# The first loads and the last batch of an attention stage, reordered, in a decoder layer on one Trainium2 core

## The reference, cut to what matters

```python
x = x + attn(layernorm(x))                      # x: 8 batches, 256 rows, 512 wide; 16 heads of 32
x = x + xattn(ctx, ctx, layernorm(x), ...)      # a convolution along the rows
x = x + ffn(layernorm(x))                       # 12 experts, top 3
# attn: q, k, v = rope(h @ Wq.T + bq), rope(h @ Wk.T + bk), h @ Wv.T + bv
#       only the first 26 and the last 64 of a batch's 256 key rows count
#       softmax(q k / sqrt(32)) @ v, then @ Wo.T + bo
```

## Time and profile before

| | |
|---|---|
| median of 3 runs | 1633.63 us (1633.26 to 1633.86) |
| the profiled execution | 1632.18 us, span 1630.4 us |
| PE busy | 1461.7 us, 90% of the span |
| POOL, DVE, ACT busy | 823.0, 795.1, 661.3 us |
| attention block | 0 to about 330 us of the span |
| first product with data on PE | 24.1 us |
| granted TensorE clock, mean | 0.936 |

### The profile page before, as it was taken

The page is one execution under the profiler, slowest core; times in us unless marked ns, Lnnn a source line. Parts: engine busy times, 40 slices in busy tenths (PEclk is TensorE's granted clock), DMA queues, the critical chain, the costliest instruction groups (busy, mean ns, idle before and its releaser), DMA issues. The chain is left out here.

```text
span 1630.4 us, 27973 instructions
## 1 busy us (share of the span) xinstructions
PE 1461.7 (90%) x7638; PEld 1113.4 (68%) x7639; DVE 795.1 (49%) x1098; ACT 661.3 (41%) x1789; POOL 823.0 (50%) x892
## 2 busy tenths in 40 slices
PE   3899999589997841999999999999999999999956
PEld 1555555357775741888888888888888888888842
DVE  3456656448888568734717443473471734000003
ACT  0545555423322130444444444544444445444420
POOL 2444555044442001576766766767666667565530
PEclk9999999989998555999999999999999999999977
DMA  6000000022233540634525433454452543241115
GB/s 243 3 1 0 0 0 1 1 74 89 83 86 113 208 161 13 188 91 110 142 64 159 106 104 100 103 161 109 103 157 50 160 103 77 50 123 32 26 23 215
DMA packets 75260, 148.08 MB, mean 91 GB/s; under 512 B 8864, under 2 KB 13472, under 8 KB 74720
## 3 DMA queue, kind: packets, MB, share of 16 engines
q1 hardware_dynamic: 59232, 110.36, 21.2%
q0 software_dynamic: 14320, 35.40, 10.6%
q10 hardware_dynamic: 1680, 1.97, 0.4%
HBM read 115.11 MB, written 32.59 MB: 91 GB/s over the span
## 5 line engine op out<-in xcount | busy, mean ns | idle before, releaser
L1481 PE MATMUL ps_h<-w_hi,xh 128*128 x708 | 250.5, 365 | 1.4 <-ACT xh L1407 1.4
L1482 PE MATMUL ps_h<-w_lo,xh 128*128 x708 | 246.0, 359 | 0.0
L1504 PE MATMUL ps_y<-w_hi,hh 128*128 x590 | 240.0, 407 | 4.4 <-issue 4.4
L1309 DVE TENSOR_TENSOR w_lo<-stage,w_hi 128x512 f32 x220 | 224.0, 1018 | 27.0
L1505 PE MATMUL ps_y<-w_lo,hh 128*128 x590 | 233.8, 396 | 0.0
L1360 POOL TENSOR_TENSOR y<-y,b_sb 128x512 f32<-128x512 f32 x59 | 80.6, 1366 | 229.6 <-ACT y L1432 229.6
L1353 POOL TENSOR_TENSOR hl<-h,hh 128x1280 fp32r<-128x1280 f32 x59 | 188.2, 3189 | 15.1 <-ACT hh L1426 15.1
L763 PE MATMUL ps_b<-kv,toe 128*128 128x320 f32 x640 | 175.2, 437 | 6.9 <-POOL kv L724 6.9
L1486 PE MATMUL ps_h<-w_hi,xl 128*128 x708 | 167.0, 357 | 0.0
L1413 ACT ACTIVATE h<-ps_h 128x512 f32<-128x512 f32 x177 | 80.6, 527 | 209.2 <-POOL hl L1353 200.8
L763 PEld LDWEIGHTS ps_b<-kv,toe 128*128 128x128 f32 x640 | 123.1, 192 | 58.9 <-issue 9.2
(11 more groups left out here) (204 smaller groups left out, 2321.2 us busy)
## 6 DMA issues: line engine op xcount, KB each, us to landing
stage<-in_wcat SPq DMA_DIRECT2D x220, 256.0 KB, 3.0
toe<-kpad SPq DMA_DIRECT2D x32, 256.0 KB, 3.2
cc<-in_ctx_rev SPq DMA_DIRECT2D x32, 192.0 KB, 3.1
w_lo<-in_wcat SPq DMA_DIRECT2D x4, 1280.0 KB, 11.5
acc<-zeros POOLq DMA_DIRECT2D x1, 4352.0 KB, 18.1
xs<-in_x SPq DMA_DIRECT2D x4, 1024.0 KB, 13.3
x2d<-xs SPq DMA_DIRECT2D x4, 1024.0 KB, 8.3
xnd<-xn_c SPq DMA_DIRECT2D x16, 256.0 KB, 2.0
```

Of the source, the lines that this page charges most:

```text
L1309: nc.vector.tensor_tensor(lo, stage[:, c % NSTAGE], hi.bitcast(F32), ALU.subtract).then_inc(split_done, 1)
L1481: nc.tensor.matmul(out, x_hi, part(w_hi, e, k * FF + lo, hi - lo), start=(k == 0), stop=False)
L1482: nc.tensor.matmul(out, x_hi, part(w_lo, e, k * FF + lo, hi - lo), start=False, stop=False)
L1504: nc.tensor.matmul(ps_y[:], h_hi, part(w_hi, e, KD * FF + k * D, D), start=(k == 0), stop=False)
```

## The change

At the start, x is loaded in the parts of `X_PARTS` (batch 0; batch 1; batches 2 and 3; batches 4 to 7), with the weights between them; ACT issues the biases only when the constants have landed. The first normalisation's statistics, aggregation and inverse root are taken in three groups (batch 0, batch 1, the rest). The inverse root is a power of -1/2 on POOL (`first_std`) in place of the square root on ACT and the reciprocal on DVE. At the end, the last batch is written out on ACT, DVE and PE: the scores of its second tile go into banks 0 to 3, once these are free, right behind those of its first tile in banks 4 to 7; its second tile's transposed probabilities are evacuated by DVE (`take_pt`) and no longer by ACT. All PSUM tiles become slices of one tile `bank`.

```diff
-        ps_t = psum("ps_t", [P, 512])
-        ps_p = psum("ps_p", [P, 2, 512])
-        ps_s = psum("ps_s", [P, 4, 512])
-        ps_o = psum("ps_o", [P, KD, P])
-
-        x_in = [sem(f"x_in{i}") for i in range(4)]
+        bank = psum("bank", [P, 8, 512])
+        ps_t = bank[:, 0]
+        ps_o = bank[:, 1].rearrange("p (k n) -> p k n", k=KD)
+        ps_p = bank[:, 2:4]
+        ps_s = bank[:, 4:8]
+
+        X_PARTS = ((0, 1), (1, 2), (2, 4), (4, B))
+        x_in = [sem(f"x_in{i}") for i in range(len(X_PARTS))]
...
-            for i in range(4):
-                sp.dma_start(xs[:, 4 * i:4 * i + 4, :], xt[:, 4 * i:4 * i + 4, :]).then_inc(x_in[i], 16)
-            for w, src, s in ((wq, wqT, wq_in), (wk, wkT, wk_in), (wv, wvT, wv_in), (wo, woT, wo_in)):
+
+            def load_x(i):
+                part = slice(TPB * X_PARTS[i][0], TPB * X_PARTS[i][1])
+                sp.dma_start(xs[:, part, :], xt[:, part, :]).then_inc(x_in[i], 16)
+
+            def load_w(w, src, done):
                 sp.dma_start(w[:].rearrange("p (k n) -> p k n", k=KD),
-                             src.rearrange("(k p) n -> p k n", p=P)).then_inc(s, 16)
+                             src.rearrange("(k p) n -> p k n", p=P)).then_inc(done, 16)
+
+            load_x(0)
+            load_w(wq, wqT, wq_in)
+            load_x(1)
+            load_w(wk, wkT, wk_in)
+            load_w(wv, wvT, wv_in)
+            load_x(2)
+            load_w(wo, woT, wo_in)
+            load_x(3)
...
+            act.wait_ge(c_in, 16)
             for t, src in ((bias_q, bq), (bias_k, bk), (bias_v, bv), (bias_o, bo)):
                 act.dma_start(t[:], src.partition_broadcast(P)).then_inc(b_in, 16)
-            act.wait_ge(var_ready, 1)
-            nc.scalar.activation(rstd[:], rstd[:], ACT.Sqrt).then_inc(std_ready, 1)
...
-            batch(B - 1, True, False, True)
-            evac_n(B - 1)
+            b = B - 1
+            exps(b, 0)
+            exps(b, 1, (0,), 0)
+            evac_pt(b, 0)
+            exps(b, 1, (1,), 0)
+            evac_o(b, 0)
+            evac_n(b - 1)
+            evac_o(b, 1)
+            evac_n(b)
...
+            def first_std(n, lo, hi):
+                pool.wait_ge(var_ready, n + 1)
+                r = rstd[:, lo:hi]
+                nc.gpsimd.tensor_tensor(r, r, power[:, lo:hi], ALU.pow).then_inc(std_ready, 1)
+
+            first_std(0, 0, TPB)
+            first_std(1, TPB, 2 * TPB)
             pool.wait_ge(c_in, 16)
             first = Steps(pool, pool_step)
             for j in range(3):
                 rope(0, j, first)
+            first_std(2, 2 * TPB, NT)
             batch(0, False, False)
...
+            steps = Steps(dve, dve_step)
+
+            def stats_of(i):
                 dve.wait_ge(x_in[i], 16)
-                with dve.Fori(4 * i, 4 * i + 4) as t:
-                    nc.vector.bn_stats(stats[:, t], xs[:, t]).then_inc(stats_done, 1)
-            dve.wait_ge(stats_done, NT)
-            for t in range(NT):
-                nc.vector.bn_aggr(mv[:, t], stats[:, t]).then_inc(aggr_done, 1)
-            dve.wait_ge(aggr_done, NT)
-            steps = Steps(dve, dve_step)
-            nc.vector.tensor_scalar(rstd[:], mv[:, :, 1], EPS, None, ALU.add).then_inc(var_ready, 1)
-            dve.wait_ge(std_ready, 1)
-            steps.do(nc.vector.reciprocal(rstd[:], rstd[:]))
-            dve.wait_ge(b_in, 64)
...
+            stats_of(0)
+            variance_of(0, TPB)
+            dve.wait_ge(std_ready, 1)
             normalise(0, 0)
             normalise(0, 1)
+            stats_of(1)
+            variance_of(TPB, 2 * TPB)
+            dve.wait_ge(std_ready, 2)
             normalise(1, 0)
             normalise(1, 1)
-            for j in range(4):
-                add_bias(0, j, bank_qkv0[j])
+            dve.wait_ge(b_in, 64)
+            add_bias(0, 0, bank_qkv0[0])
+            add_bias(0, 1, bank_qkv0[1])
+            stats_of(2)
+            add_bias(0, 2, bank_qkv0[2])
+            stats_of(3)
+            variance_of(2 * TPB, NT)
+            add_bias(0, 3, bank_qkv0[3])
+            dve.wait_ge(std_ready, 3)
             dve.wait_ge(taps_in, 32)
...
-            batch(B - 1, True, False, True, tail)
+
+            def take_pt(f):
+                dve.wait_ge(pt_done, 4 * B - 1 + f)
+                if f == 0:
+                    dve.wait_ge(pv_done, 2 * B - 1)
+                nc.vector.tensor_copy(view(pT[:], f * 8 * P, [[4 * P, 2], [1, 4 * P]]), ps_s[0:NK, 2 * f:2 * f + 2])\
+                    .then_inc(pt_evac_last, 1)
+
+            b = B - 1
+            softmax_top(b, 0, tail)
+            softmax_top(b, 1, tail, 0)
+            variance(b - 1)
+            softmax_sum(b, 0, tail)
+            softmax_sum(b, 1, tail, (0,))
+            normalise_1(b - 1)
+            take_pt(0)
+            softmax_sum(b, 1, tail, (1,))
+            take_pt(1)
+            residual(b, 0, True, tail)
+            evac_n(b - 1)
+            residual(b, 1, True, tail)
...
-            batch(B - 1, True, False, True)
-            n_t(B - 1, 0)
-            n_t(B - 1, 1)
+
+            def four_banks_free():
+                pe.wait_ge(t_evac, t_qk(B - 1, 2) + 1)
+                pe.wait_ge(p_evac, p_wo(B - 2, 1, False) + 1)
+                pe.wait_ge(o_evac, 2 * B - 1)
+
+            b = B - 1
+            scores(b, 0)
+            scores(b, 1, four_banks_free, 0)
+            p_t(b, 0, 0)
+            p_t(b, 0, 1)
+            pe.wait_ge(exp_done, 4 * b + 3)
+            p_v(b, 0)
+            pe.wait_ge(pt_evac, 4 * b + 2)
+            p_t(b, 1, 0)
+            n_t(b - 1, 0)
+            pe.wait_ge(exp_done, 4 * b + 4)
+            w_o(b, 0, True)
+            pe.wait_ge(pt_evac, 4 * b + 3)
+            p_t(b, 1, 1)
+            n_t(b - 1, 1)
+            p_v(b, 1, True)
+            w_o(b, 1, True)
+            n_t(b, 0)
+            n_t(b, 1)
...
```

More of the change, by code:

```diff
@@ L128, in attention @@
         rstd1 = sb("rstd1", [P, TPB])
-        power = sb("power", [P, TPB])
+        power = sb("power", [P, NT])
         turn = sb("turn_a", [P, 1])
@@ L158, in attention @@
         pt_evac = sem("pt_evac")
+        pt_evac_last = sem("pt_evac_last")
         pv_done = sem("pv_done")
@@ L246, in evac_k, with exps @@
                 evac(qkt_done, 3 * b + 3, kT[:], ps_t[:].rearrange("p (k n) -> p k n", k=KD)[:, :, 0:NK])
-            def exps(b, t):
-                for f in range(2):
+            def exps(b, t, halves=(0, 1), at=4):
+                for f in halves:
                     act.wait_ge(nmx_ready, 4 * b + 2 * t + f + 1)
@@ L338, in inverse_std @@
                 pool.wait_ge(var1_ready, b + 1)
-                nc.gpsimd.tensor_tensor(rstd1[:], rstd1[:], power[:], ALU.pow).then_inc(rstd1_ready, 1)
+                nc.gpsimd.tensor_tensor(rstd1[:], rstd1[:], power[:, 0:TPB], ALU.pow).then_inc(rstd1_ready, 1)
             def repeat(b, t):
@@ L373, in _, with variance_of @@
         def _(dve):
-            for i in range(4):
+            steps = Steps(dve, dve_step)
+            def stats_of(i):
                 dve.wait_ge(x_in[i], 16)
-                with dve.Fori(4 * i, 4 * i + 4) as t:
-                    nc.vector.bn_stats(stats[:, t], xs[:, t]).then_inc(stats_done, 1)
-            dve.wait_ge(stats_done, NT)
-            for t in range(NT):
-                nc.vector.bn_aggr(mv[:, t], stats[:, t]).then_inc(aggr_done, 1)
-            dve.wait_ge(aggr_done, NT)
-            steps = Steps(dve, dve_step)
-            nc.vector.tensor_scalar(rstd[:], mv[:, :, 1], EPS, None, ALU.add).then_inc(var_ready, 1)
-            dve.wait_ge(std_ready, 1)
-            steps.do(nc.vector.reciprocal(rstd[:], rstd[:]))
-            dve.wait_ge(b_in, 64)
+                for n in range(TPB * X_PARTS[i][0], TPB * X_PARTS[i][1]):
+                    nc.vector.bn_stats(stats[:, n], xs[:, n]).then_inc(stats_done, 1)
+            def variance_of(lo, hi):
+                dve.wait_ge(stats_done, hi)
+                for n in range(lo, hi):
+                    nc.vector.bn_aggr(mv[:, n], stats[:, n]).then_inc(aggr_done, 1)
+                dve.wait_ge(aggr_done, hi)
+                nc.vector.tensor_scalar(rstd[:, lo:hi], mv[:, lo:hi, 1], EPS, None, ALU.add).then_inc(var_ready, 1)
             def settle():
@@ L419, in softmax_top, with softmax_sum @@
                                             ALU.mult).then_inc(nmx_ready, 1)
-            def softmax_sum(b, t, steps):
-                for f in range(2):
+            def softmax_sum(b, t, steps, halves=(0, 1)):
+                for f in halves:
                     dve.wait_ge(exp_done, 4 * b + 2 * t + f + 1)
@@ L556, in w_o, with scores @@
                 mm.then_inc(wo_done, 1)
-            def scores(b, t):
+            def scores(b, t, free=None, at=4):
                 if t == 0:
                     pe.wait_ge(t_evac, t_qk(b, 2) + 1)
-                pe.wait_ge(pt_evac, 4 * b + 2 * t + 1)
+                if free is None:
```

(12 more changed lines are left out.)

6 lines of the change are left out of this document (3 added, 3 removed).

## The result

| | before | changed |
|---|---|---|
| median | 1633.7 us (1633.26 to 1633.86, 4 runs) | 1616.59 us (1614.73 to 1619.98, 4 runs) |
| profiled execution, span | 1632.18, 1630.4 us | 1614.73, 1612.8 us |

The ratio is 0.9898, 95% interval 0.988 to 0.9916: 17.1 us, where 13.3 were forecast. I compare the two profiled executions, 17.45 us apart.

The account below looks back on a forecast made before the run. The prediction took the attention block's two ends as the bound: the wait for all of x and the last batch's chain. 11.9 + 1.4 = 13.3 us off 1633.63 gives 1620.3 us, range 1617.2 to 1624.5.

Parts of the forecast that it names:

- both mechanisms: Attention block: batch 0 starting without all of x gains 11.9 us; the last batch's reordered scores and evacuation gain 1.4.
- S: Start of batch 0's exponentials on ACT, forecast at 41.8 us instead of 53.68, 11.9 us gained.
- Step (b): Start, DVE: last x lands at 29.8 us, eight statistics take 5.1, twelve aggregations 0.9; POOL starts at 36.2.
- Step (c): Start, POOL: the power over 12 columns takes 2.8 us (0.29 + 12 x 0.207), ending at 39.0.
- Step (d): Start: DVE adds at 39.0 us, `kpad` lands at 40.9, `evac_x(1, 1)` lasts 0.88 to 41.8; the 1.28 table load goes.
- The loop behind keeps its waits and its length.: Behind the start of batch 0's exponentials, the attention loop was claimed to keep its waits and its length.
- PE's 3 us of waiting in batch 0: Batch 0: PE on its own would move 14.8 us earlier, the exponentials 11.9, so PE waits about 3 us.
- The end: Last batch: the last output projection comes at 316.9 us instead of 318.33, 1.4 us gained.
- The rival of the clock: Last batch: PE's lower clock lasts into the output projection, the end gives nothing, 1621.7 us; chance 0.15.
- one of the signs of being wrong that the prediction names: The prediction is wrong if the granted clock is at 0.50 in the loop or at the last batch's projections.
- The median: Whole kernel: the median was put 1.45 us above the profiled execution, so 1620.3 us rather than 1618.9.

Follow-up runs that it names:

- e8_power_twice: The changed kernel with a second power over 12 columns on POOL, on a spare tile, ahead of the third group's; 1619.21 us, ratio 0.9916.
- e10_one_root: The changed kernel with one unread square root of one column on ACT, bringing back the table load ahead of batch 0's exponentials; 1621.2 us, ratio 0.9931.
- e2_end_only: The changed kernel with the start put back as in the kernel before, so only the change at the end remains; 1629.81 us, ratio 0.9982.
- e0_again: The changed kernel timed once more with nothing edited; 1617.64 us, ratio 0.9907 to the kernel before.
- e5_pe_kept_busy: The changed kernel with nine unread matrix products in PE's gaps, at the block's end and the convolution's start; 1614.52 us, ratio 0.989.
- e9_all_and_busy_start: The changed kernel with late power wait, last x ahead of wo, last batch's scores first, nine spare products, and three in batch 0; 1606.65 us, ratio 0.9851.

## Why the prediction was wrong

Its direction, both mechanisms and every link of the chain up to S were right; the sum was 3.8 us short (4.2 between the two profiled executions), by terms that were mis-sized and by one it did not have.

- **Step (b), the landing and the statistics.** Landing 29.14 us, not 29.8; eight statistics in 4.85 us, not 5.1. POOL started at 35.3 instead of 36.2. The price of 0.636 a tile came from twelve rows with a wait among them; four tiles without one took 2.47 us before, 0.62 each, and written out they are 0.61.
- **Step (c), the power over 12 columns.** 2.28 us, not 2.8: 0.158 us a column beyond the first two, not 0.207. The row of one column that I took for the fixed part was an addition's. The estimate by the Trainium skill that I weighed against it (GPSIMD Engine Reference, section 3.1), which has 2.6 cycles an element for a two-input operation, would have been 0.73; the measurement decides against it for a power.
- **Step (d).** `kpad` and the rest of the chain held: issue 0.17 us after the addition, 1.7 to its landing. From `evac_x(1, 1)`'s start to the exponential's it took 0.75 us and not 0.88: the exponential starts before the evacuation has ended, which the table load did not do. With (b) and (c) S came to 40.26 and not 41.8: 1.5 of the missing us. e8_power_twice and e10_one_root show that the power and the dropped table load stand on this path in full, and the 11.10 us from the last x to the exponentials in six profiles that the landing does. A part of this term is chance: the landing moved by 1.9 us between executions of the same loads.
- **"The loop behind keeps its waits and its length."** This step failed. Behind S the changed kernel gained another 1.34 us, 1.19 of it in batch 0. The profile of before had PE itself as a second bound there: its q projections, 8.58 us long at the low clock, ended just before both halves' transposes, which ran back to back. e2_end_only, with the same start, had 7.41 us and a batch 0 of 30.16. Of these 1.1 us PE gives 0.33 directly; the other 0.8 is DVE's division of the second tile, 1.77 us long behind POOL's start and 0.96 ahead of it. The changed kernel has the same two differences (0.34 at the k projection, 0.91 for the division). So 1.1 us of the gain is the kernel before having had a long stretch at 1.2 GHz in the profiled execution; whether its other executions had it no trace shows.
- **PE's 3 us of waiting in batch 0.** They did not appear. PE's own part moved by 15.05 us (q projections from 51.20 to 36.15), and its q projections, again at the low clock (8.95 us), filled the time until the first transposes of the probabilities at 44.94.
- **The end.** 2.0 us instead of 1.4: 24 exponentials took 7.46 us (281.25 to 288.71) and both `evac_pt` 1.99, where I had 7.57 and 2.1, and neighbours on ACT overlap, so the first output projection came 0.4 us earlier; from there to the last one it was 7.75 us, not 7.9. The rival of the clock was real: at 0.50 into the projections in e0_again, it took 4.0 us, more than the end brings. I had it at 0.15; of the changed kernel's three profiles it was one. That is also one of the signs of being wrong that the prediction names.
- **Behind the block.** The sum ended there. The profiles have another 0.9 us: 0.4 lost where the convolution starts and 0.7 won in it (181.99 us, 182.68 before), where the granted clock left 0.50 sooner behind its first product, and 0.6 in the feed-forward part, whose cause is open.
- **The median.** I put it 1.45 us above the profiled execution, as before; it was 1.86 above. Over the twelve executions of the changed kernel the median is 1616.7, and its gains over the kernel beside it were 17.1, 14.9 and 16.2 us: about 16, still more than the 13.3. The range was too narrow by the spread of either kernel, which three runs within 0.6 us did not show; with the 14.9 us alone the sum would have looked better, by luck.

## What to carry to other kernels

When a first stage is cut loose from a load, look for what in the program's order still waits for the last byte: here the landing of x, eight statistics and a power stood ahead of a small transfer that released ACT, and moving one wait behind it brought the exponentials 2.0 us closer to the last x. Where two waits end close together, as S and PE's projections, price both: the second caps the gain, and it moved with the clock. A shift of a few tenths of a us can grow where two engines' instructions meet: 0.33 us became 1.13, as it decided whether DVE or POOL began first. In these profiles a gap of some us on PE was paid twice, in the gap and in what ran at the low clock behind it. Three spare products in batch 0's gap gave it back 2.0 us in the one profile taken; behind the last work of the block they cost 1.2 us in e5_pe_kept_busy, where they ran at the low clock, and nothing in e9_all_and_busy_start, where they didn't.

## What the runs showed of the hardware

A power on POOL took 0.69 to 0.73 us over 128x2 and 2.28 over 128x12. A division of 128x720 on DVE took 0.91 and 0.96 us where it began ahead of POOL's two-input operation over 90x512, which then took 1.82 us (changed kernel and e2_end_only); where POOL's began first, the division took 1.77 us and POOL's 1.16 (kernel before). The last part of x, in six profiles with the same order of loads, let DVE's first statistic start between 28.89 and 30.76 us. The same code met the low clock for different lengths: q's sixteen matmul records of batch 1, the kernel before and e2_end_only having the same start, took 8.58 and 7.41 us, and the last output projection 3.67 or 5.37 behind the same gap of 5.86 us earlier in the batch. Single executions of the changed kernel lay up to 5.3 us apart, the three profiled ones 4.2, in which the traces show differences in the granted clock and in this landing. With three spare products between batch 0's first transposes of q and k the granted clock stayed at 1.00 through batch 0 (e9_all_and_busy_start, one profile), where in every other profile it fell to 0.50.
